# Flamingo-style decoder layers on one core: rows normalised one step earlier, expert sums brought in four batches ahead, layer 1's base through DRAM

## What is computed

```
x = x + tanh(g_xattn[0]) * xattn0(layernorm(x), ctx, mask0)
x = x + tanh(g_ffn[0])   * moe(layernorm(x))            # top 2 of 8 experts, F = 1024
x = x + tanh(g_xattn[1]) * xattn1(layernorm(x), ctx, mask1)
x = x + tanh(g_ffn[1])   * real(ifft(fft(layernorm(x)) @ w)) + gate * bias
# xattn: q = x Wq', k = ctx Wk', v = ctx Wv'; softmax((q k' masked) / 4) v, then Wo'
# moe:   softmax of the gate, two largest renormalised; up * gelu(gate), down
...
```

## Time and profile before

| | |
|---|---|
| median of 3 runs | 1344.51 us (1343.1 to 1349.46) |
| the profiled execution's own time | 1344.64 us |
| its span, first to last instruction | 1343.1 us |
| granted TensorE clock, mean share of full | 0.931 |
| busy: PE, DVE, ACT, POOL | 84%, 65%, 44%, 21% |
| start-up, to layer 0's first scores | 0 to 76.9 us |
| layer 0's first `residual` to its 14th | 101.3 to 347.3 us |
| experts, about | 408 to 995 us |
| layer 1's first `residual` to its 14th | 1063.4 to 1302.1 us |

### The profile page before, as it was taken

The page is one execution under the profiler, slowest core; times in us unless marked ns, Lnnn a source line. Parts: engine busy times, 40 slices in busy tenths (PEclk is TensorE's granted clock), DMA queues, the critical chain, the costliest instruction groups (busy, mean ns, idle before and its releaser), DMA issues.

```text
span 1343.1 us, 32603 instructions
## 1 busy us (share of the span) xinstructions
PE 1124.6 (84%) x10697; PEld 944.7 (70%) x10698; DVE 868.1 (65%) x2583; ACT 593.2 (44%) x1251; POOL 280.7 (21%) x383
## 2 busy tenths in 40 slices
PE   5178778787778999999999999999996778878886
PEld 3166667666657878788887878888874666666664
DVE  4057766767856666575766767675565577777773
ACT  3156655556624242332424242332233565666663
POOL 6302433433342000000000000000013233344410
PEclk9588988889878999999999999999997899999998
DMA  8754555545538513131220313100024344444430
GB/s 253 238 136 124 158 150 142 149 129 153 170 136 280 210 45 106 42 101 47 70 89 32 116 40 119 40 29 29 25 86 123 99 113 121 119 122 113 121 82 25
DMA packets 143662, 150.55 MB, mean 112 GB/s; under 512 B 41418, under 2 KB 111280, under 8 KB 141433
## 3 DMA queue, kind: packets, MB, share of 16 engines
q1 hardware_dynamic: 122982, 82.97, 22.9%
q0 software_dynamic: 14960, 57.44, 12.8%
q10 hardware_dynamic: 5616, 8.78, 1.8%
HBM read 80.80 MB, written 58.84 MB: 104 GB/s over the span
## 4 chain that ended last, share of the span: by engine, by line
PE 63%; DVE 11%; ACT 9%; issue 7%; DMA 5%; POOL 2%; ACTq 2%; SPq 1%; DVEq 0%; another core or an unknown queue 0%; POOLq 0%
PE bank L1978 25%; PE bank L1991 13%; PE bank L1797 6%; PE bank L1664 4%; PE bank L1644 3%; DVE bm L1279 3%; ACT h L966 2%; ACT pr L1005 2%; PE bank L1732 2%; PE bank L1740 2%; ACT pr L1004 2%; DMA query_halves<-qT 2%; PE bank L1808 1%; DVE pr L525 1%; ACT hT L957 1%
## 5 line engine op out<-in xcount | busy, mean ns | idle before, releaser
L1978 PE MATMUL bank<-tiles,we 128*128 128x256 f16 (+1 forms) x3744 | 393.7, 259 | 5.8 <-issue 4.9
L1978 PEld LDWEIGHTS bank<-tiles,we 128*128 128x128 f16 x3744 | 325.3, 98 | 46.4 <-issue 13.4
L1143 ACT ACTIVATE tiles<-bank 128x256 f32<-128x256 f32 (+1 forms) x312 | 109.3, 353 | 333.5 <-PE bank L1978 302.9
L1991 PE MATMUL bank<-we,tiles 128*128 128x256 f16 x1608 | 224.1, 274 | 16.2 <-DVE tiles L1576 15.5
L1572 DVE SCALAR_TENSOR_TENSOR tiles<-bank,tiles 128x256 f32<-128x256 f32 (+1 forms) x312 | 119.9, 384 | 158.3 <-ACT tiles L1143 153.7
L1991 PEld LDWEIGHTS bank<-we,tiles 128*128 128x128 f16 x1608 | 147.8, 98 | 53.5 <-DVE tiles L1576 29.1
L1004 ACT ACTIVATE pr<-bank 116x512 f32<-116x512 f32 x192 | 108.9, 567 | 103.3 <-PE bank L1740 99.4
L1279 DVE TENSOR_REDUCE bm<-bank 128x6 bf16<-128x462 f32 (+1 forms) x192 | 105.2, 578 | 61.1 <-PE bank L1708 59.9
L1578 DVE TENSOR_TENSOR tiles<-tiles 128x256 f16<-128x256 f32 (+1 forms) x312 | 121.1, 388 | 11.1 <-DVE tiles L1576 0.5
L525 DVE TENSOR_TENSOR pr<-pr 116x512 f16<-116x512 f32 x160 | 109.1, 683 | 25.6 <-ACT pr L1005 23.0
L1732 PE MATMUL bank<-qop,kop 125*116 125x256 f16 (+1 forms) x352 | 98.8, 303 | 18.2 <-ACT pr L1005 16.2
(11 more groups left out here) (204 smaller groups left out, 1697.9 us busy)
## 6 DMA issues: line engine op xcount, KB each, us to landing
qop<-query_halves SPq DMA_DIRECT2D x96, 144.0 KB, 3.2
wes<-in_guT POOLq DMA_DIRECT2D x9, 1024.0 KB, 5.1
query_halves<-qT SPq DMA_DIRECT2D x32, 256.0 KB
expert_out<-zeros POOLq DMA_DIRECT2D x4, 2048.0 KB, 17.9
tiles<-expert_in SPq DMA_DIRECT2D x29, 256.0 KB, 2.7
pr<-in_guT POOLq DMA_DIRECT2D x7, 1024.0 KB
yg<-in_dnT POOLq DMA_DIRECT2D x7, 1024.0 KB, 6.4
expert_out<-tiles ACTq DMA_DIRECT2D x28, 256.0 KB, 2.1
```

What stands on the lines that cost most here:

```text
L1978: last = pe.matmul(bank[1 + fc % 3][:, half * S:half * S + w * P], gate_up[:, par, c, i, col:col + P], xT[:, j, c, 0:w * P], start=n == 0, ...
L1991: last = pe.matmul(bank[4 + t][:, 0:D], act16[:, fc % 4, i, t * P:(t + 1) * P], we[:, par, 2, j, fc * D:(fc + 1) * D], start=fc == 0 and n ...
```

## The change

It is one change of the hand-written order with several parts:

- **Third batch ahead.** `pre_stats`, `root`, `pre_norm` and `h_norm` are now for batch b+3 in step b (`third(b)`), not b+2. `t_h` and `h_hi` stay at b+2 and move forward: PE turns right behind `proj_o`, ACT copies right behind `expo(b, 1)`. `proj_q` follows `values(b, 1)`.
- **DVE's order.** `pre_stats` stands behind `maxima` 0 and 1, `pre_norm` behind `maxima` 2 and 3; `place` and `q_low` move forward; `w_low(b, 5)` stands behind the last `maxima`.
- **Loads and sums four ahead.** `load`, `gather` and `combine` are for b+4 in step b, `recall` for b+5. On POOL two gathers stand first in the step and two behind both roots.
- **The base through DRAM.** `store_sum` writes `xin` to a DRAM table, `base` reads it from there.
- **The start.** 16 small padding DMAs become 3 for layer 0, and 3 for layer 1 in step 1; late masks and layer 1's weights are loaded behind the first batches' queries, the Fourier tables in step 1; two roots stand ahead of the small bias loads on POOL; the counts of the late masks move from the start to the end of step 0.
- **Loop.** The rolled part begins one step earlier.

```diff
@@ steps @@
-    step(at(layer, 2), True, True, True, True)
     with eng.Fori(0, 5) as j:
+        step(Batch(layer, j * 2 + 2, j + 1, 0), True, True, True, True)
         step(Batch(layer, j * 2 + 3, j + 1, 1), True, True, True, True)
-        step(Batch(layer, j * 2 + 4, j + 2, 0), True, True, True, True)
+    step(at(layer, 12), True, True, True, False)
     step(at(layer, 13), True, True, True, False)
...
+def third(b):
+    return not (isinstance(b.i, int) and b.i > NB - 4)
@@ SP @@
-                src = rows(x_d, b.i * S) if b.layer == 0 else xin[:, b.par]
+                if b.layer:
+                    sp.wait_ge(s_sum[b.par], 16 * (b.own + 1))
+                src = rows((x_d, x2_d)[b.layer], b.i * S)
                 sp.dma_start(xb[:, b.par], src).then_inc(s_base[b.par], 16)
+            def store_sum(b):
+                sp.wait_ge(s.combine_step, b.i * 3 + 3)
+                sp.dma_start(rows(x2_d, b.i * S), xin[:, b.par]).then_inc(s_sum[b.par], 16)
...
             load_maxima(at(0, 0))
             sp.wait_ge(s.keys_stored, 32 * 3 * KC)
-            sp.wait_ge(s.mask_flags, 5)
+            load_late()
...
@@ POOL step @@
                 if part:
-                    wait_apart(pool, s.places_recalled, b.i + 4)
-                if part:
-                    gather(b.after(3), 0)
-                if pre:
-                    root(b.after(2))
-                if part:
-                    gather(b.after(3), 1)
-                    gather(b.after(3), 2)
+                    wait_apart(pool, s.places_recalled, b.i + 5)
+                    gather(b.after(4), 0)
+                    gather(b.after(4), 1)
                 if tail:
                     ln_root(1, s.root_after, s.variance_after, pv)
+                if third(b):
+                    root(b.after(3))
                 if part:
-                    gather(b.after(3), 3)
+                    gather(b.after(4), 2)
+                    gather(b.after(4), 3)
@@ ACT step @@
-                for g in range(1, 5):
-                    expo(b, g)
+                expo(b, 1)
                 if pre:
-                    h_norm(b.after(2))
                     h_hi(b.after(2))
+                expo(b, 2)
+                expo(b, 3)
+                if pre:
+                    q_hi(b.after(2))
+                expo(b, 4)
+                if tail:
+                    h2_norm(pv)
+                if front:
+                    v_spread(nx, 0)
                 expo(b, 5)
...
+                if third(b):
+                    h_norm(b.after(3))
@@ DVE step @@
                 w_low(b, 0)
-                if pre:
-                    pre_stats(b.after(2))
                 w_low(b, 1)
...
                 if tail:
                     update_stats(pv)
-                if pre:
-                    pre_norm(b.after(2))
+                if b.layer == 0 and not (isinstance(b.i, int) and b.i < 2):
+                    place(b.after(-2))
                 w_low(b, 3)
+                if pre:
+                    q_low(b.after(2))
+                if tail:
+                    renorm(pv)
                 if front:
                     maxima(nx, 0)
                     maxima(nx, 1)
...
+                if third(b):
+                    pre_stats(b.after(3))
                 w_low(b, 4)
...
-                    recall(b.after(4))
-                    combine(b.after(3))
+                    recall(b.after(5))
+                    combine(b.after(4))
                 normalise(b)
@@ layer 1's entry, DVE @@
+            recall(at(1, 3))
+            combine(at(1, 2))
+            pre_stats(at(1, 2))
             for g in range(GP):
                 maxima(at(1, 0), g)
-            combine(at(1, 2))
-            recall(at(1, 3))
+            pre_norm(at(1, 2))
+            recall(at(1, 4))
+            combine(at(1, 3))
@@ PE step @@
                     proj_o(pv)
+                if pre:
+                    t_h(up2)
                 values(b, 0)
                 scores(b, 3)
                 values(b, 1)
...
```

More of the change, by code:

```diff
@@ L656, in step0 @@
                 if ld:
-                    if not tail:
-                        sp.wait_ge(s.normed, 2)
-                    load(b.after(3))
+                    sp.wait_ge(s.normed, b.n + 3)
+                    load(b.after(4))
                 clear(b)
@@ L751, in step1 @@
             def step1(b, front, tail, pre, ld):
+                if third(b):
+                    store_sum(b.after(3))
+                if ld:
+                    sp.wait_ge(s.normed, b.n + 3)
+                    sp.wait_ge(s_sum[b.par], 16 * (b.after(2).own + 1))
+                    load(b.after(4))
                 if not (isinstance(b.i, int) and b.i < 2):
@@ L786, in _ @@
             load_keys(at(1, 0), 0)
-            base(at(1, 0))
+            load_keys(at(1, 0), 1)
+            store_sum(at(1, 0))
+            sp.wait_ge(s.normed, NB + 1)
+            sp.wait_ge(s_sum[0], 16)
+            load(at(1, 2))
+            load_keys(at(1, 1), 0)
+            load_keys(at(1, 1), 1)
             store_queries(at(1, 0))
@@ L802, in _ @@
                 store_keys(1, m, 2)
+            store_sum(at(1, 2))
             load_maxima(at(1, 0))
@@ L1104, in _ @@
             m_out(at(0, 0))
+            h_norm(at(0, 2))
             bulk_high(0, 12)
@@ L1203, in _ @@
             v_spread(at(1, 0), 1)
+            h_norm(at(1, 2))
             m_out(at(1, 0))
@@ L1403, in step @@
                     maxima(nx, 1)
-                if tail:
-                    renorm(pv)
-                if b.layer == 0 and not (isinstance(b.i, int) and b.i < 2):
-                    place(b.after(-2))
+                if third(b):
+                    pre_stats(b.after(3))
                 w_low(b, 4)
@@ L1411, in step @@
                     maxima(nx, 3)
-                if pre:
-                    q_low(b.after(2))
-                w_low(b, 5)
+                if third(b):
+                    pre_norm(b.after(3))
                 if front:
@@ L1427, in step @@
                         finish(pv)
+                if b.layer == 0 and isinstance(b.i, int) and b.i == 0:
+                    open_rows(4, NB, b_small)
                 if b.layer == 0 and isinstance(b.i, int) and b.i == 0:
@@ L1481, in _ @@
             q_low(at(0, 1))
+            pre_stats(at(0, 2))
             bulk_low(0, 7)
@@ L1864, in step @@
                     proj_q(up2)
+                scores(b, 4)
+                values(b, 2)
+                if b.layer == 0 and isinstance(b.i, int) and b.i == 1:
+                    pe.wait_ge(s.unmasked_rows, 2)
                 if front:
-                    top_scores(nx, 3)
+                    top_scores(nx, 0)
+                    top_scores(nx, 1)
                 if ranked:
                     pe.wait_ge(s.ranks_read, b.i - 1)
+                if front:
+                    spread(nx, 0)
+                scores(b, 5)
+                values(b, 3)
+                if front:
+                    top_scores(nx, 2)
+                    top_scores(nx, 3)
+                    pe.wait_ge(s.values_spread, 2 * nx.n + 1)
                 if tail:
                     t_h2(pv)
+                values(b, 4)
                 if front:
                     top_scores(nx, 4)
-                values(b, 4)
-                if front:
                     top_scores(nx, 5)
```

142 lines of the change are left out of this document (68 added, 74 removed).

## The result

The changed kernel takes 1399.88 us (median of 4 runs, 1398.45 to 1403.62); the forecast was 1394. The kernel before took 1343.8 us in the same comparison, so the ratio is 1.0414 (95% interval 1.0377 to 1.0452): slower by 4%.

What follows compares the result with a forecast made beforehand. PE was read as busiest with DVE close behind, the start-up as bound by DMAs. 1344.6 - 15 (start) + 11 (layer 0) + 3 (layer 1's entry) + 50 (layer 1) = 1394 us; range 1344 to 1428.

Steps and rivals of the forecast that it cites:

- Layer 1, +50: Layer 1's steps: two gathers behind the later root delay combine; 17.55 to about 21.75 us in 12 steps.
- `combine`'s wait: Layer 1: DVE was to wait 3 us or so for the gather's DMA in each of 12 steps.
- The third rival, "slower still: the clock": PE runs layer 1's t_att, proj_o, t_h at 1.2 GHz, up to 2.7 us a step: 1426 us; chance 0.18.
- Layer 0, +11: Layer 0's steps: h_hi delays w_low(b, 2) and DVE's list; 18.6 against 17.7 us, 12 times.
- with durations of rows 6: Layer 0's step was priced from one step read in detail, which ran undisturbed at 17.7 us.
- The start, -15: Start-up: batch 0's residual at 83 to 90 us where it was at 101.3; bounds -29 and -8.
- the first scores at 44.8: Start-up: layer 0's first scores, at 76.90 us before, were to begin near 45 us.
- Layer 1's entry, +3: Layer 1's entry: a root, four gathers and two combines delay step 0's first w_low; bounds 0 and +8 us.
- The base through DRAM at nothing: Layer 1: store_sum and base through DRAM add 256 KB per batch, costed at nothing; about 2 us a step if uncovered.
- the missing wait of L1644 for L966: A sign of a right forecast: no wait of source line L1644 for L966 would be left.
- DVE's wait in step 0: Layer 0, step 0: DVE was to wait some 13 us for POOL's root of batch 3.
- the removed wait: PE's largest single wait inside a step, for h_norm: 16.9 us in 11 steps, 1.5 each, to go with the change.

Runs made afterwards that it cites:

- hhi: The changed kernel with h_hi moved behind expo(b, 2) on ACT in both layers; ratio 1.029 to the kernel before.
- start: The changed kernel with POOL's expert-weight fetch and zero writes at the end of its step 0, behind batch 3's root; ratio 1.041.
- g4: The changed kernel with all four gathers of batch b+4 ahead of both roots on POOL, layer 1 only; ratio 1.033.
- stats: The changed kernel with only pre_stats(b+3) moved back between w_low(b, 0) and w_low(b, 1) on DVE; ratio 1.002.
- start2: Changed kernel, gathers first, h_hi behind expo(b, 2), pre_stats heading DVE's list, and POOL's fetch and zeros at the end of step 1; ratio 0.965.
- dram: The kernel before the change, with only layer 1's base going by way of DRAM; ratio 1.001.
- fill: The changed kernel with PE repeating spread(b+1, 0)'s two products ten times and spread(b+1, 1)'s five times; 1424.8 us, ratio 1.060.

## Why the prediction came out right, and where it did not

*Layer 1, +50, measured +26.* The mechanism was there step by step, and it set the step (`t_att` 0.05 us behind `att` in all 12): `w_low(b, 2)` at 5.6 us behind `t_att` (forecast 5.95), `pre_stats` done at 11.3 (11.5), two gathers behind the second root, `combine` waiting 2.7 us (over 3). Two sizes were off. The last gather landed 17.5 us behind `t_att`, not 18.4 to 18.9: it needed 3.0 us where I took 3.62, and was issued a little sooner. That made the step 20.6 us, not 21.75: 14 us in 12 steps. And I compared with the undisturbed step of 17.55, while the 13 steps before had run at 18.4 on average: 0.8 x 13, the other 10 us. The new steps are nearly all alike. `hhi` and `start` have 20.5 to 20.6 in layer 1 as well, with `combine`'s wait at the end of the path there too.

*What the term left out* is that the wait was not the only bound. `g4` took it away and the step hardly moved, 0.75 us. The third rival, "slower still: the clock", had a part of the mechanism: PE was at its lower level in 10 of the 12 steps. I gave it `t_att`, `proj_o` and `t_h`, added to the wait; in the trace it was the Fourier product and `scores`, *beside* the wait, and `t_att` and `proj_o` behind it ran at the full level (1.03 us for four matmuls in the step shown). The two overlap, and so the sum was not 1426.

*Layer 0, +11, measured +28.7.* The step that failed is "with durations of rows 6": the undisturbed step, at the full level. I had kept the clock for layer 1. By the trace, layer 0 fell to the lower level in nearly every step (0.89 to 0.72), and `scores`, `t_att`, `proj_o` and `t_h` took so long that ACT stood up to 4.4 us before the copy and `w_low(b, 2)` started at 10.0 to 11.1 us, not 7.85. DVE's list behind it was as I had added it up. What the copy costs by itself the runs leave open (up to 13.8 us, `hhi`); the place of `pre_stats` costs 19 to 33 us (`stats`) for a 0.94 us operation, which I had booked at its own duration. Why PE fell to the lower level, and so how the place of `pre_stats` costs that much, no run separates.

*The start, -15, measured -2.8.* The mechanism held (the first scores at 44.8, DVE waiting for POOL's root behind the zeros), its sizes did not: the late masks landed at 61 and not at 50, so the wait was 16.9 and not 13 us and ended some 8 us later, and the bias rows, which I had let land between 80 and 87, landed at 95. `start` and `start2` show what holds them: the zeros, wherever they are put.

*Layer 1's entry, +3, measured +2.9*: the number is right for the whole stretch from layer 0's 14th `residual` to layer 1's first. From the 16th it is +5.5, and layer 0's last two steps gave 2.6 back; what of this the entry cost is not shown. *The base through DRAM at nothing*: right by `dram`.

*The signs.* `combine`'s wait, the missing wait of L1644 for L966 (now L1696 for L1005), DVE's wait in step 0 (16.9 us for 13) and the first scores at 44.8 came as said. The steady steps did not: 20.6 us in layer 1 where I had 21 to 23, and 22.1 in layer 0 where I had 18.5 to 20. Nor was `att` the largest wait of PE's matmuls in layer 1: 7.0 us, behind 11.1 for `maxima`.

*The chances.* That the time came within 6 us of the forecast is luck: three errors, +18, +12 and -24, that cancel. What the forecast rested on, that late work on POOL and DVE costs more than the removed wait gave, is shown; which piece of late work counts most, it had wrong: I had put the weight on the gathers (9.8 us by `g4`) and the least on `pre_stats` (21 in layer 1, 19 to 33 in layer 0).

## What to carry to other kernels

In an in-order list, the place of a small operation can count for more than its duration: the same 0.94 us cost 3 us a step more between the `maxima` than at the head of DVE's list. To judge a wait, look at what else is ready at the moment it ends: 2.7 us of waiting were worth 0.75 here, because PE was ready in the same tenth of a microsecond in most steps. And where a trace shows PE at its lower level in some steps, price the new step at both levels: the term for layer 0, priced at the full one alone, came out at less than half.

## What was not expected of the hardware

- The clock made small delays large: the same four matmuls took 1.03 or 1.91 us, and in a step where 0.94 us of DVE time was moved out of the way, 2.1 us more went from `t_mask` to `t_att`, with 379 ns a matmul for 634.
- Steps of the same code lasted 22.2 us in one kernel and 20.4 in another that differs only ahead of them (and ran on another chip), and steady steps of different code (layer 0 of `hhi` and `start`) both 20.4 to 20.6. In both the granted clock was at the lower level for half of each step, at the same place in it. An edit worth less than such a jump may show nothing, or all of it.
- A DMA of 6 KB (the bias rows) took 2.35 us alone, 6.7 and 12.8 us with 5 MB of zero writes issued just ahead, and the row of maxima 14.9.
- A gather of 128 KB landed 3.0 us after its start in the changed kernel's step, 3.62 in the earlier trace rows.
- Whether thin work on PE is what lowers its clock stays open: `fill` raised the clock and not the speed, and every other edit that raised it also shortened the step.
